# Causal attention: the triangle added by TensorE for all diagonal blocks of the first two query chunks

## The chip, the cores and the metric

The kernel runs on one core of one Trainium2 chip. The metric is the device time of one execution in microseconds (us). The kernel before took 1374.01 us, the median of three runs (1373.12 to 1380.39).

## The reference, cut to what matters

The whole computation has six blocks on 2048 tokens of width 128: a gated feed-forward, a causal attention, the feed-forward again, a mixture of experts, a full attention and the mixture again. The change is in the causal attention alone (16 heads of width 8, all 2048 tokens):

```
scores = jnp.einsum('bhqd,bhkd->bhqk', q, k) * (1.0 / np.sqrt(HD))
causal = (jnp.arange(t)[:, None] >= jnp.arange(t)[None, :]).astype(scores.dtype)
scores = scores * causal - (1.0 - causal) * NEG
attn = jax.nn.softmax(scores, axis=-1)
out = jnp.einsum('bhqk,bhkd->bhqd', attn, v)
```

## The kernel before

The causal attention works in 32 windows: four query chunks `c` of 512 queries, and for each chunk eight pairs of heads, so windows 0 to 7 are chunk 0, 8 to 15 chunk 1, and so on (`Plan.windows`, line 882). Each window is done twice over. First come the row maxima. A `fill` (lines 1245 to 1270) takes one tile of 128 queries, `qt` from 0 to 3, and one key chunk `kc` up to the own one. TensorE computes the scores of both heads into two PSUM banks (line 1262), a head on each half of the array's rows, and VectorE reduces both banks to a maximum per query (lines 1433 to 1443). In the own key chunk only the columns up to the diagonal are computed, so a fill is 128, 256, 384 or 512 wide for `qt` 0 to 3, and its last 128 columns need the triangle that hides later keys. For `qt` 2 and 3 TensorE adds it with four small matmuls (line 1268: identity halves against `hide_q`, accumulated into the same banks), and VectorE does one plain reduction over both banks (line 1441). For `qt` 0 and 1 VectorE does it: one `tensor_tensor_reduce` for each of the two heads adds `mask_q` while it takes the maximum (line 1435); it is a custom operation and a read of the accumulator in the trace. After the last fill of a window one small reduction gives `negmax` (line 1449), POOL splits it into three bf16 parts (lines 1465 to 1471), and TensorE's `turn` adds them to the queries (lines 1281 and 1284), which ScalarE copies to `q_max` (line 1405).

Second come the probabilities, in steps of 128 keys. `scores` (line 1300) fills one of three PSUM banks per head, ScalarE takes the exponential (line 1414), POOL clears what lies under the diagonal of diagonal steps (line 1484), and TensorE multiplies with the values three steps later (`sum_values`, line 1319). ScalarE keeps the sums of a window at the third step of the next (line 1388), and SP sends them to DRAM. Keys and queries of chunk 1 are loaded from DRAM in front of the loop; those of chunks 2 and 3 when the sums of windows 8 and 16 are kept (line 1557).

All engines follow one list, `Plan.order`, written by `in_time` (lines 966 to 1008), a small planner that keeps a clock for TensorE (`tensor`), VectorE (`vector`) and ScalarE (`scalar`), each in us. At each turn it puts down what can start first: a fill (from the time that VectorE's clock minus 1.2 allows), a turn (5 us after the window's maxima), or a step. A fill may be at most six windows ahead of the steps (`AHEAD`). TensorE waits at fill `u` until VectorE has used fill `u - 2` (line 1258), and takes everything in the order of the list. The costs that the planner charges a fill are these:

```
tensor = first + 0.08 + width / 3500.0 + (0.2 if own and late else 0.0)
vector = max(vector, tensor + 0.2) + (0.45 if own and not late else 0.11) + 2 * width / 960.0
```

where `own` says that the key chunk is the query chunk's own and `late` that TensorE adds the triangle. A step costs `tensor` 0.33 us and its columns (up to 512) by 1/4500 + 1/1200 each, and a turn costs it 0.6. The last fill of a window adds 0.2 to `vector`. The full attention further on uses the same classes with `causal` false; its order comes from `in_turns`, and no fill of it is masked.

Of the kernel before, what the change touches and what calls it, by code (L numbers as in the profile page):

```python
# [874 lines left out]
class Plan:  # L875
# [30 lines left out]
    def fills(self, n):  # L906
# [3 lines left out]
            return [(q, j, CW) for j in range(NC) for q in range(TPC)]  # L910
        return [(q, j, CW if j < c else TW * (q + 1)) for q in range(TPC) for j in range(c + 1)]

    def first_query(self, n, kt):

        r = kt - TPC * self.windows[n][1]
        return (TW * r, True) if self.causal and r >= 0 else (0, False)
# [49 lines left out]
    def in_time(self):  # L966


        settle, margin = 5.0, 1.6
        order, tensor, vector, scalar = [], 0.0, 0.0, 0.0  # L970
        maxed, turned, begun = {}, {}, set()
        f = t = turn = 0
        while t < len(self.steps):
            n, i = self.steps[t]
            at_fill = at_turn = at_step = math.inf
            if f < len(self.steps) and self.steps[f][0] < n + self.AHEAD:
                at_fill = max(vector - 1.2, tensor)
            if turn in maxed and (turn < 2 or turn - 1 in begun):
                at_turn = max(maxed[turn] + settle, tensor)
            if n in turned:  # L980
                at_step = max(scalar - 0.5, turned[n] + margin, tensor)
            first = min(at_fill, at_turn, at_step)
            if first == at_turn:
                order.append(("turn", turn, 0))
                turned[turn] = first
                tensor = first + 0.6
                scalar = max(scalar, tensor + 0.2) + 0.6
                turn += 1
            elif first == at_fill:
                m, g = self.steps[f]  # L990
                width = self.fills(m)[g][2]
                order.append(("fill", m, g))
                own, late = self.fills(m)[g][1] == self.windows[m][1], self.fills(m)[g][0] >= 2
                tensor = first + 0.08 + width / 3500.0 + (0.2 if own and late else 0.0)
                vector = max(vector, tensor + 0.2) + (0.45 if own and not late else 0.11) + 2 * width / 960.0
                f += 1
                if g == self.keys(m) - 1:
                    maxed[m] = vector
                    vector += 0.2
            else:  # L1000
                q0, _ = self.first_query(n, i)
                order.append(("exp", n, i))
                begun.add(n)
                tensor = first + 0.2 + (CW - q0) / 4500.0 + 0.13 + (CW - q0) / 1200.0
                scalar = max(scalar, first + 0.5) + 0.3 + 2 * (CW - q0) / 1400.0 + 0.4 / self.keys(n)
                t += 1
        assert f == len(self.steps) and turn == self.count
        return order


class Attention:
# [216 lines left out]
    def pe_loop(self, pe):  # L1228
        ps, k, plan, causal, ST, SUM, MX, NP = self.ps, self.k, self.plan, self.causal, self.ST, self.SUM, self.MX, self.NP
# [15 lines left out]
        def fill(m, f):  # L1245
            u = plan.fill_no[m, f]
            qt, kc, width = plan.fills(m)[f]
            pair, c = plan.windows[m]
            if f == 0:
                operands(m)  # L1250
            if causal and u == 1:
                pe.wait_ge(self.rest_ready, 2 * NC)
            if not causal and m == 0:
                pe.wait_ge(self.k_built, kc + 1)
                if f == 1:
                    pe.wait_ge(self.stage_norm.out, NC * self.stage_ln + NC)
            if u >= 2:
                pe.wait_ge(self.mx_used, u - 1)
            q0 = CW * c + TW * qt
            for j in range(2):  # L1260
                head = slice(HALF * j, HALF * j + HALF)
                mm = pe.matmul(ps[:, MX + 2 * (u % 2) + j, 0:width], q_all[head, pair, q0:q0 + TW],  # L1262
                               k_all[head, pair, CW * kc:CW * kc + width], start=True, stop=True)
            if causal and kc == c and qt >= 2:
                for h in range(2):
                    for j in range(2):
                        head = slice(HALF * j, HALF * j + HALF)
                        mm = pe.matmul(ps[:, MX + 2 * (u % 2) + j, width - TW:width], k["ident_h"][head, h, :],
                                       k["hide_q"][head, h, :], start=False, stop=True, skip_group_check=True)
            mm.then_inc(self.mx_filled, 1)  # L1270
# [149 lines left out]
    def dve_loop(self, dve):  # L1420
        nc, ps, k, plan, MX = self.nc, self.ps, self.k, self.plan, self.MX
        blockmax, negmax = k["blockmax"], k["negmax"]
        for kind, m, f in plan.order:
            if kind == "queries":
                self.dve_rest(dve, m)
            elif kind == "end":
                self.dve_end(dve, m, f)
            if kind != "fill":
                continue
            u = plan.fill_no[m, f]  # L1430
            qt, kc, width = plan.fills(m)[f]
            dve.wait_ge(self.mx_filled, u + 1)
            if self.causal and kc == plan.windows[m][1] and qt < 2:
                for j in range(2):
                    reduce = nc.vector.tensor_tensor_reduce(  # L1435
                        k["hidden"][:, u % 2, j, 0:width], ps[:, MX + 2 * (u % 2) + j, 0:width],
                        k["mask_q"][:, 2 * TW - width:], 1.0, LOWEST, ALU.add, ALU.max,
                        blockmax[:, m % plan.AHEAD, qt, j, kc:kc + 1])
                reduce.then_inc(self.mx_used, 1)
            else:  # L1440
                nc.vector.tensor_reduce(blockmax[:, m % plan.AHEAD, qt, :, kc],  # L1441
                                        ps[:, MX + 2 * (u % 2):MX + 2 * (u % 2) + 2, 0:width], AX.X, ALU.max)\
                    .then_inc(self.mx_used, 1)
            if f == len(plan.fills(m)) - 1:
                dve.wait_ge(self.mx_used, u + 1)
                if m >= plan.AHEAD:
                    dve.wait_ge(self.max_split, 4 * (m - plan.AHEAD + 1))
                blocks = plan.windows[m][1] + 1 if self.causal else NC
                nc.vector.tensor_reduce(negmax[:, m % plan.AHEAD, :, :], blockmax[:, m % plan.AHEAD, :, :, 0:blocks],  # L1449
                                        AX.X, ALU.max, negate=True).then_inc(self.max_ready, 1)  # L1450
                if m % PAIRS == PAIRS - 1 and m > PAIRS:
                    self.dve_invert(dve, m // PAIRS - 1)
# [527 lines left out]
```

## Time and profile before

| what | value |
|---|---|
| median of three runs | 1374.01 us (1373.12 to 1380.39) |
| span of the profiled execution, its own time | 1378.3 us |
| TensorE matmul busy | 1310.4 us, 95% |
| VectorE busy | 1163.7 us, 84% |
| ScalarE busy | 1054.2 us, 76% |
| POOL busy | 164.8 us, 12% |
| masked reductions (L1435) | 128, in the causal attention |
| plain block reductions (L1441) | 768, in both attentions |

The profiled execution is one more execution of the same program; its span is the only time the page has for it. Busy time counts what an engine was at work on; matmuls are pipelined, so their durations overlap and a start to start time says more than a duration. The loop of the causal attention lies between about 85 and 464 us. Idle time is given with what ended it.

### The profile page before, as it was taken

To read this page: it belongs to the slowest core of one execution; us is meant where nothing else is said; L and a number is where in the kernel's file an instruction comes from. 1 tells how busy PE (TensorE), PEld (TensorE's weight loads), DVE (VectorE), ACT (ScalarE), POOL (GpSimd) and SP (SyncE) were. 2 spreads that over 40 slices of the span, in tenths; PEclk is the share of its full clock that TensorE was granted. 3 is DMA by queue.
4 is the path that set the end of the run, shared out by engine and by line. 5 is a ranking of instruction groups with operands and counts; after the bars stand their busy time and mean duration, and the time that the engine had idled before them with its cause. 6 is when DMAs were issued, how large, how long until landed. Compare 5 with 4: busy or idle time off the path is not lost.

```text
span 1378.3 us, 30094 instructions
## 1 busy us (share of the span) xinstructions
PE 1310.4 (95%) x11833; PEld 473.9 (34%) x11896; DVE 1163.7 (84%) x1536; ACT 1054.2 (76%) x2060; POOL 164.8 (12%) x443
## 2 busy tenths in 40 slices
PE   7888999999999898999899999999999999999999
PEld 4343333332333452534233333332333323333533
DVE  6878889999998278555899999999999999995554
ACT  4557888988999546324499999999999999998521
POOL 9234222111111000001000000000000000000000
PEclk9999999999999999899699999999999999999989
DMA  5252301100000012001311000000000000000000
GB/s 147 51 136 40 54 12 36 28 4 12 4 4 4 12 37 56 0 0 52 109 50 49 4 3 12 4 4 3 12 4 3 4 8 9 3 4 3 11 6 25
DMA packets 38524, 35.09 MB, mean 25 GB/s; under 512 B 16080, under 2 KB 31920, under 8 KB 38384
## 3 DMA queue, kind: packets, MB, share of 16 engines
q1 hardware_dynamic: 38384, 33.17, 9.9%
q8 instruction: 94, 1.54, 0.5%
q14 instruction: 46, 0.38, 0.1%
HBM read 17.03 MB, written 9.70 MB: 19 GB/s over the span
## 4 chain that ended last, share of the span: by engine, by line
DVE 32%; PE 21%; issue 1%; ACT 0%; DVEq 0%; ACTq 0%
DVE m_blockmax L1441 31%; PE ps L1323 6%; PE ps L1262 3%; PE ps L1300 3%; PE ps L630 1%; PE ps L619 1%; PE ps L620 1%; PE ps L252 0%; PE ps L245 0%; PE ps L1075 0%; PE ps L1166 0%; PE ps L605 0%; PE ps L648 0%; DVE m_negmax L1449 0%; PE ps L1213 0%
## 5 line engine op out<-in xcount | busy, mean ns | idle before, releaser
L1441 DVE TENSOR_REDUCE m_blockmax<-ps 128x2 f32<-128x1024 f32 (+1 forms) x768 | 880.8, 1207 | 26.6 <-PE ps L1262 18.1
L1414 ACT ACTIVATE m_prob<-ps 128x512 f32<-128x512 f32 (+3 forms) x1664 | 845.9, 577 | 48.0 <-PE ps L1300 33.6
L1300 PE MATMUL ps<-m_q_max,m_k_all 64*128 64x512 bf16 (+3 forms) x1664 | 338.2, 368 | 0.5
L1262 PE MATMUL ps<-m_k_all,m_q_all 64*128 64x512 bf16 (+3 forms) x1664 | 317.8, 380 | 19.9 <-DVE m_blockmax L1441 15.3
L1323 PE MATMUL ps<-m_prob,m_v_op 128*16 128x256 f32 x4096 | 321.0, 385 | 0.1
L1262 PEld LDWEIGHTS ps<-m_k_all,m_q_all 64*128 64x128 bf16 x1664 | 79.8, 93 | 343.2 <-DVE m_blockmax L1441 174.8
L1319 PE MATMUL ps<-m_prob,m_v_op 128*16 128x256 f32 (+3 forms) x2560 | 179.3, 352 | 1.5 <-ACT m_pv L1388 0.8
L1300 PEld LDWEIGHTS ps<-m_q_max,m_k_all 64*128 64x128 bf16 x1664 | 143.3, 94 | 90.5 <-ACT m_prob L1414 47.5
L1323 PEld LDWEIGHTS ps<-m_prob,m_v_op 128*16 128x16 f32 x4096 | 67.4, 94 | 133.5 <-issue 101.3
L1465 POOL CAST m_maxparts<-m_negmax 128x8 bf16<-128x8 f32 x64 | 14.0, 218 | 719.8 <-DVE m_negmax L1449 714.6
L729 ACT ACTIVATE m_prob<-ps 128x512 f32<-128x512 f32 x40 | 23.6, 594 | 74.4 <-PE ps L619 74.4
L1319 PEld LDWEIGHTS ps<-m_prob,m_v_op 128*16 128x16 f32 x2560 | 42.3, 94 | 79.9 <-issue 51.6
L1405 ACT ACTIVATE m_q_max<-ps 128x512 bf16<-128x512 f32 x64 | 38.2, 597 | 38.6 <-PE ps L1284 38.4
L1484 POOL TENSOR_SCALAR_AFFINE_SELECT m_prob<-m_prob 128x256 f32<-128x256 f32 x128 | 51.3, 407 | 129.6 <-ACT m_prob L1414 128.1
L814 DVE TENSOR_TENSOR m_prob<-m_prob,ps 128x512 f32<-128x512 f32 x32 | 22.0, 689 | 32.5 <-PE ps L648 31.6
L1435 DVE CUSTOM_DVE_ANT_0 m_hidden<-ps,m_mask_q 128x256 bf16<-128x256 f32 (+1 forms) x128 | 39.8, 351 | 2.3 <-PE ps L1262 2.0
L260 DVE COPY m_cen<-ps 128x512 f32<-128x512 f32 x28 | 19.0, 685 | 23.3 <-ACT m_sq L288 17.6
L619 PE MATMUL ps<-m_xn,m_e_gate 128*128 128x512 f32 x64 | 35.4, 637 | 2.8 <-DVE m_prob L814 2.6
L292 ACT ACTIVATE m_std<-ps,m_eps 32x128 f32<-32x128 f32 x28 | 10.0, 357 | 34.1 <-PE ps L245 34.1
L1132 POOL TENSOR_TENSOR m_part<-m_sq,m_part 128x512 bf16<-128x512 f32 x8 | 9.2, 1154 | 224.6 <-ACT m_part L1107 224.6
L237 PE MATMUL ps<-m_x,m_centre_of 128*128 128x512 f32 x42 | 25.2, 701 | 10.6 <-DVE m_x L518 5.5
L630 PE MATMUL ps<-m_prob,m_e_down 128*128 128x512 f32 x64 | 35.3, 638 | 0.0
(221 smaller groups left out, 1034.8 us busy)
## 6 DMA issues: line engine op xcount, KB each, us to landing
m_part<-m_xn SPq DMA_DIRECT2D x48, 128.0 KB, 2.3
ba_parts<-m_part SPq DMA_DIRECT2D x8, 384.0 KB, 4.7
ea_parts<-m_part SPq DMA_DIRECT2D x8, 384.0 KB, 2.6
m_k_all<-ea_parts SPq DMA_DIRECT2D x84, 32.0 KB
m_q_all<-ea_parts SPq DMA_DIRECT2D x84, 32.0 KB
m_k_all<-ba_parts SPq DMA_DIRECT2D x36, 64.0 KB
m_q_all<-ba_parts SPq DMA_DIRECT2D x36, 64.0 KB
ba_sums<-m_pv SPq DMA_DIRECT2D x128, 9.0 KB
```

Of the source, the lines that this page charges most:

```text
L237: pe.matmul(self.ps[:, bank, :], self.k["centre_of"][:, :], chunk(src, c), start=True, stop=True)\
L619: pe.matmul(ps[:, i % 2, :], wg, chunk(xn, c), start=True, stop=True).then_inc(self.gate_done, 1)
L630: pe.matmul(ps[:, self.DOWN + m % 2, :], wd, k["hid"][:, i % 2, :], start=(shared or g == 0), stop=(shared or g == GROUPS - 2)).then_inc(s ...
L1262: mm = pe.matmul(ps[:, MX + 2 * (u % 2) + j, 0:width], q_all[head, pair, q0:q0 + TW], k_all[head, pair, CW * kc:CW * kc + width], start=Tr ...
L1300: pe.matmul(ps[:, e % ST, q0:CW], k_all[head, pair, TW * i:TW * i + TW], q_max[m % 2][head, q0:CW], start=True, stop=True).then_inc(self.s ...
L1319: mm = pe.matmul(ps[VC * g:VC * g + VW, SUM, HALF * first:HALF_CW], weights, own, start=(i == 0), stop=True, skip_group_check=True)
L1323: mm = pe.matmul(ps[VC * g:VC * g + VW, SUM, 0:HALF_CW], weights, own, start=(i == 0), stop=True, skip_group_check=True)
L1405: nc.scalar.activation(q_max[m % 2][:, :], ps[:, e % ST, :], ACT.Copy).then_inc(self.st_used, 1)
L1414: nc.scalar.activation(prob[:, (2 * t + j) % NP, q0:CW], ps[:, e % ST, q0:CW], ACT.Exp, scale=SCALE)\
L1435: reduce = nc.vector.tensor_tensor_reduce(k["hidden"][:, u % 2, j, 0:width], ps[:, MX + 2 * (u % 2) + j, 0:width], k["mask_q"][:, 2 * TW - ...
L1441: nc.vector.tensor_reduce(blockmax[:, m % plan.AHEAD, qt, :, kc], ps[:, MX + 2 * (u % 2):MX + 2 * (u % 2) + 2, 0:width], AX.X, ALU.max)\
L1484: pool.affine_select(out=own, in_=own, compare_op=ALU.is_ge, fill=0.0, base=0, pattern=[[0, 2], [1, TW]], channel_multiplier=-1).then_inc( ...
```

## The change

One new function says which fills TensorE masks: those of `qt` 2 and 3 as before, and now also those of `qt` 0 and 1 in windows of chunks 0 and 1. TensorE's fill, VectorE's loop and the planner's costs ask it in place of `qt >= 2` and `qt < 2`.

```diff
+    def masked_by_tensor(self, n, qt):
+
+        return qt >= 2 or self.windows[n][1] < 2
+
...
-                own, late = self.fills(m)[g][1] == self.windows[m][1], self.fills(m)[g][0] >= 2
+                own, late = self.fills(m)[g][1] == self.windows[m][1], self.masked_by_tensor(m, self.fills(m)[g][0])
...
-            if causal and kc == c and qt >= 2:
+            if causal and kc == c and plan.masked_by_tensor(m, qt):
...
-            if self.causal and kc == plan.windows[m][1] and qt < 2:
+            if self.causal and kc == plan.windows[m][1] and not plan.masked_by_tensor(m, qt):
```

## Rows read from the trace of the kernel before

**Rows 1.** The page: the span, and busy time, share and instructions of each engine.
```profile
span 1378.3 us, 30094 instructions
...
PE 1310.4 (95%) x11833; PEld 473.9 (34%) x11896; DVE 1163.7 (84%) x1536; ACT 1054.2 (76%) x2060; POOL 164.8 (12%) x443
```

**Rows 2.** Busy time by stretch of the causal loop, the columns in the second line.
```profile
core 0: us, PE busy (x) PEld busy (x) DVE busy (x) ACT busy (x) POOL busy (x), PEclk, DMA share, GB/s
107.00:133.00 26.00, 23.89 (x340) 9.82 (x344) 22.36 (x57) 21.45 (x59) 13.24 (x45) 1.00 0.20 39
133.00:140.00 7.00, 5.26 (x64) 2.02 (x64) 6.17 (x10) 4.27 (x12) 1.71 (x7) 1.00 0.04 8
140.00:205.00 65.00, 60.67 (x755) 20.98 (x762) 57.80 (x107) 54.64 (x127) 16.82 (x53) 1.00 0.25 35
205.00:218.00 13.00, 10.66 (x124) 3.71 (x124) 12.75 (x20) 8.52 (x21) 2.28 (x8) 1.00 0.02 5
...
328.00:434.00 106.00, 104.80 (x1226) 33.78 (x1224) 103.31 (x139) 97.43 (x204) 15.01 (x48) 1.00 0.03 7
```

**Rows 3.** ScalarE's timeline (start, length): the keeping of a window's sums.
```profile
106.69 0.38 ACT L1388 ACTIVATE m_pv<-ps 128x256 f32<-128x256 f32 x1
...
133.04 0.38 ACT L1388 ACTIVATE m_pv<-ps 128x256 f32<-128x256 f32 x1
139.85 0.39 ACT L1388 ACTIVATE m_pv<-ps 128x256 f32<-128x256 f32 x1
...
204.91 0.41 ACT L1388 ACTIVATE m_pv<-ps 128x256 f32<-128x256 f32 x1
217.50 0.38 ACT L1388 ACTIVATE m_pv<-ps 128x256 f32<-128x256 f32 x1
...
310.63 0.39 ACT L1388 ACTIVATE m_pv<-ps 128x256 f32<-128x256 f32 x1
327.27 0.38 ACT L1388 ACTIVATE m_pv<-ps 128x256 f32<-128x256 f32 x1
```

**Rows 4.** VectorE's timeline, 210 to 214 us: two masked fills and what follows each.
```profile
210.58 0.29 DVE L1435 CUSTOM_DVE_ANT_0 m_hidden<-ps,m_mask_q 128x128 bf16<-128x128 f32 x1 [0.21 <-PE ps L1262]
...
211.01 2.35 DVE L1441 TENSOR_REDUCE m_blockmax<-ps 128x2 f32<-128x1024 f32 x2
213.28 0.41 DVE L1435 CUSTOM_DVE_ANT_0 m_hidden<-ps,m_mask_q 128x256 bf16<-128x256 f32 x1
...
213.96 5.48 DVE L1441 TENSOR_REDUCE m_blockmax<-ps 128x2 f32<-128x1024 f32 x5
```

**Rows 5.** VectorE's plain reductions by shape, 84 to 442 us: busy, mean ns, idle before.
```profile
L1441 DVE TENSOR_REDUCE m_blockmax<-ps 128x2 f32<-128x1024 f32 x224 | 263.5, 1219 | 17.7 <-PE ps L1262 14.0 <-PE ps L1268 1.9
L1441 DVE TENSOR_REDUCE m_blockmax<-ps 128x2 f32<-128x768 f32 x32 | 30.5, 952 | 4.3 <-PE ps L1268 4.0
```

**Rows 6.** The chain that ended last: five full reductions in a row.
```profile
1048.88 5.73 DVE m_blockmax L1441 x5
```

**Rows 7.** Timeline around a masked fill 384 wide: fill, masks, next scores.
```profile
152.48 0.34 PE L1262 MATMUL ps<-m_k_all,m_q_all 64*128 64x384 bf16 x2
...
152.65 0.28 PE L1268 MATMUL ps<-m_hide_q,m_ident_h 64*128 64x128 bf16 x4
...
152.77 0.27 PE L1300 MATMUL ps<-m_q_max,m_k_all 64*128 64x256 bf16 x2
```

**Rows 8.** Timeline, chunk 1: second weight load of the scores behind a fill 128 wide.
```profile
157.39 0.09 PEld L1300 LDWEIGHTS ps<-m_q_max,m_k_all 64*128 64x128 bf16 x1 [0.21 <-ACT m_prob L1414]
```

**Rows 9.** Timeline, chunk 0: the exponentials behind a fill 256 wide issued at 112.06.
```profile
112.60 1.09 ACT L1414 ACTIVATE m_prob<-ps 128x512 f32<-128x512 f32 x2 [0.53 <-PE ps L1300]
```

**Rows 10.** Busy time by stretch, columns as in rows 2; the DMA share is next to last.
```profile
112.00:114.00 2.00, 1.84 (x28) 0.89 (x27) 1.79 (x10) 1.18 (x4) 0.81 (x3) 1.00 0.58 123
114.00:116.00 2.00, 1.93 (x32) 0.78 (x28) 1.95 (x6) 1.95 (x5) 1.38 (x6) 1.00 0.10 20
```

**Rows 11.** TensorE's timeline: the first fill of chunk 1, window 8.
```profile
119.67 0.39 PE L1262 MATMUL ps<-m_k_all,m_q_all 64*128 64x512 bf16 x2 [0.32 <-DVE m_blockmax L1441]
```

## The prediction

> **What bounds the kernel now.** I read the page first, then the busy time by stretch, then the moments at which each window's sums are kept, and last the timeline around single fills. The page [rows 1] shows a span of 1378.3 us with TensorE busy 95% and VectorE 84%. Neither share decides anything here: the change touches only the causal attention, whose loop runs from about 85 to 464 us, and within it only the blocks of chunks 0 and 1. The second attention takes its order from another function and stays as it is, as does all that follows.
>
> By stretch [rows 2]: in chunk 0 (107 to 133 us) and chunk 1 (140 to 205 us) no engine is full. VectorE works 22.36 of 26.00 and 57.80 of 65.00 us, ScalarE 21.45 and 54.64. In chunk 3 (328 to 434 us) VectorE works 103.31 of 106.00 us and sets the pace. Between chunks 0 and 1 (133 to 140 us) ScalarE works only 4.27 of 7.00 us, and between 1 and 2 (205 to 218 us) only 8.52 of 13.00, while VectorE has 12.75 of 13.00. There the planned order issues fills without exponentials, because the first window of the next chunk needs more maxima than are ready: VectorE is late and ScalarE starves.
>
> The keeping of the sums once per window gives these **stalls** a size [rows 3]. Six windows of chunk 0 take 26.35 us, 4.39 each; the seventh interval takes 6.81, of which some 0.2 is that it holds two wider steps: stall 2.2. Seven of chunk 1 take 65.06 us, 9.29 each; the next takes 12.59: stall 3.3. Seven of chunk 2 take 93.13 us, 13.30 each; the next 16.64: stall 3.3. Together 8.8 us. The reader is to see that the loop loses at its chunk borders what VectorE could have done ahead in chunks 0 and 1, where from 107 to 205 us it idles 98.00 - 22.36 - 6.17 - 57.80 = 11.7 us [rows 2].
>
> **The change part by part.** It moves 32 fills (8 pairs, 2 chunks, the query tiles 0 and 1) from a pair of masked reductions on VectorE to four mask matmuls on TensorE and one plain reduction.
>
> VectorE, removed: of a 128 wide fill the pair takes 211.01 - 210.58 = 0.43 us, of a 256 wide one 213.96 - 213.28 = 0.68 us, with the reads of the accumulator inside [rows 4]. Added: a plain reduction over 256 or 512 elements, of which the trace has none. The rows have 1219 ns for 1024 and 952 ns for 768 [rows 5], so 1.04 ns an element; carried on, 418 and 685 ns. In a queue without gaps five of them take 5.73 us [rows 6], that is (5.73 - 1.22) / 4 = 1.13 us apart, 0.09 under the duration. So the new ones cost 0.33 and 0.60 us, and each fill saves 0.10 and 0.08 us: 32 fills, 2.9 us of VectorE. By itself it is off the path in chunks 0 and 1, where VectorE idles 11.7 us, and so worth nothing there. Ends: nothing, and 2.9 us if all of it reaches the path.
>
> TensorE, added: 128 matmuls. Behind a 384 wide fill the first mask starts at 152.65 and the scores behind the fourth at 152.77: 0.12 us for four [rows 7]. Two row halves of the array run side by side. Upper end: the whole 0.28 us of that group's row, since a 128 wide fill hides less of the four weight loads. I take 0.12, as it is a start to start time in the same queue. On the path? In chunk 1 the scores behind a fill mostly wait for ScalarE to free a buffer: the second weight load of the scores at 157.39 waited 0.21 us for it [rows 8], more than 0.12, so there I cost the masks at nothing; the cover is ScalarE's queue, and without it 16 x 0.12 = 1.9 us would come on top. In chunk 0 ScalarE stands idle for 0.53 us until the scores behind a 256 wide fill arrive [rows 9], so there the 8 tiles 1 pay 8 x 0.12 = 1.0, and the 8 tiles 0 half: 0.5. Term: +1.5 us.
>
> The TensorE page of the Trainium skill ("TensorE: Matmul & The Clock Gate", section "Wait - 56ns, not 53.3ns?") speaks against this change: with hardware decode off the sequencer spends about 62 ns on each matmul, which binds when the array's work is shorter. That would be 128 x 62 ns = 7.9 us in place of 32 x 0.12 = 3.8. This trace does not agree: its four matmuls take 0.12 us from start to start.
>
> The order, moved: the planner is told the new costs, and this is the larger part. It charged a masked fill with 0.45 + 2 x width / 960: 0.72 and 0.98 us, where the rows have 0.43 and 0.68. It now charges 0.11 + the same: 0.38 and 0.64, near the 0.33 and 0.60 above. Over 32 fills its VectorE clock falls by 32 x 0.34 = 10.9 us, and its TensorE clock rises by 32 x 0.2 = 6.4. A fill goes into the order when the planned VectorE has at most 1.2 us left, so in chunks 0 and 1 fills move ahead of exponentials. Per window of chunk 0 (fills of 128 + 256 + 384 + 512 = 1280 columns) the planner now sums 2 x 1280 / 960 + 4 x 0.11 + 0.2 = 3.3 us of VectorE against 4.8 of TensorE (before: 4.0 against 4.4), in chunk 1 8.0 against 9.1 (before 8.7 and 8.7). The old order runs 15 fills ahead of the exponentials through chunk 1, 19 through chunk 2 and 23 in chunk 3, and wins the four more at each border by letting the exponentials wait. Now this lead has time to grow before the border. That fills the 11.7 us of VectorE's idle time, and the stalls shrink. I take the first two as gone and the third as halved, because in chunk 2 nothing is cheaper and the lead can only be kept: 2.2 + 3.3 + 1.6 = 7.1 us. What is moved costs TensorE its time in the steady part: some 8 fills at 0.24 us (two halves of 512 columns side by side, against the 2 x 128 columns in 0.12 us above) are now issued between exponentials: 1.9 us. Needed of VectorE: 7.1 of the 11.7 us of idle.
>
> What is late next: TensorE takes fills in order, so a fill ahead of VectorE holds the scores behind it, and ScalarE with them. Fills of chunk 1 need their keys from DRAM. The DMA engines are 0.58 busy from 112 to 114 us and 0.10 from 114 to 116 [rows 10], so that load has landed by 114 to 115; its first fill is issued at 119.67 [rows 11] and would move ahead by some 3 to 4 us. The cover is 1 us thin; without it TensorE stands up to 1 us. POOL's maxima splits, SP's sends and loads are as many as before and follow the same events.
>
> **Sum:** +1.5 (masks) +1.9 (moved fills) -7.1 (stalls) = **-3.7 us**. The profiled execution's span of 1378.3 us is 4.3 above the median of 1374.01, within the runs' 1373.12 to 1380.39; I put the difference on the median: 1374.0 - 3.7 = **1370.3 us**. A measurement of this kernel can tell about 0.5%, 6.9 us, from no change; so this forecast, -0.3%, counts as no change.
>
> **Rivals.**
> Full use of the idle time. The new plan is near the truth for VectorE, so all 11.7 us of idle and the 2.9 us saved turn into an earlier end: 14.6 - 1.5 - 1.9 = 11.2 us, 1362.8. For it: chunk 3 is set by VectorE [rows 2], so what is ahead at its start counts to the end. Against it: the exponentials need TensorE and ScalarE, and their steady periods do not fall. Chance 0.22.
>
> No lead gained. The fills are placed earlier, but TensorE waits for VectorE in front of them and pays at each window what it wins at the border. Then only the masks are left, 0 to 3.8 us, middle 1.5: 1375.5. For it: chunk 0's windows are short chains through four engines. Chance 0.20.
>
> Slower: the narrow fills do not hide the four weight loads and the sequencer, so each of the 32 pays the 0.28 us of the group [rows 7], and VectorE gets its block as much later: 32 x 0.28 = 9.0 us, 1383.0 with no stall won. It decides if the group's time, not the start to start time, is what the next instruction waits for; against it stands 152.77 itself. The Trainium skill's 62 ns a matmul (same page and section) would come to 7.9 us, much the same place. Chance 0.10.
>
> That the change does nothing is excluded: the test holds for every window of chunks 0 and 1, and both loops and the planner ask it.
>
> **How the numbers follow.** Forecast 0.48, with its own range 1366 to 1374 (all three stalls gone, or one of them only). Range: from 1363.0, most of the full use, to 1377.5, the masks with no cover. It leaves out the slower case and a little of the full one. Faster by over 0.5% (under 1367.1): all of full use, 0.22, and 0.12 of the forecast: 0.34. Slower by over 0.5% (over 1380.9): 0.10 and a little for chunk 1's load and a worse order: 0.11. Same: the rest, 0.55.
>
> **What would show it.** Masked custom operations down from 128 to 64; plain reductions 32 more, at 0.42 and 0.69 us. Mask matmuls up by 128. The intervals 6.81 and 12.59 us near 4.8 and 9.5, the third below 16. VectorE's idle time from 107 to 205 us near 5 in place of 11.7. The last sums at about 460 in place of 464.2 us. I am wrong if chunk 0's windows grow by over 0.5 us each, if the stalls stay, or if anything behind the loop moves.

## The result, and the profile after

The changed kernel takes 1388.83 us, the median of 22 runs (1379.39 to 1397.06). Beside them on the same chips the kernel before took 1381.99 us (22 runs, 1373.12 to 1390.36; the three runs that were shown ahead of the prediction lie at the low end of these). The ratio is 1.0046, 95% interval 1.0025 to 1.0066: slower by 0.46%, between 0.25 and 0.66%. The forecast was -0.3%. Of the 18.5 us between its 1370.3 and the measured 1388.83, 8.0 are this difference of the kernel before (1381.99 against 1374.01).

The profile that follows is of the slowest of the 22 executions (1397.06 us).

The page of the changed kernel, its span, engines and two groups of section 5 (the first is VectorE's plain reduction, the second TensorE's fill; behind the bar stand busy time, mean ns and the idle time ahead of them):

```profile
span 1395.3 us, 30317 instructions
...
PE 1326.0 (95%) x12024; PEld 472.2 (34%) x12024; DVE 1163.0 (83%) x1440; ACT 1057.3 (76%) x2060; POOL 165.0 (12%) x443
...
L1445 DVE TENSOR_REDUCE m_blockmax<-ps 128x2 f32<-128x1024 f32 (+3 forms) x800 | 896.8, 1181 | 44.3 <-PE ps L1266 33.3
...
L1266 PE MATMUL ps<-m_k_all,m_q_all 64*128 64x512 bf16 (+3 forms) x1664 | 318.4, 381 | 30.5 <-DVE m_blockmax L1445 20.7
```

VectorE has fewer instructions and as much busy time as before (1163.7) [rows 1], and its reductions now wait longer for fills: of the causal loop, VectorE's plain reductions by shape, 84 to 456 us:

```profile
L1445 DVE TENSOR_REDUCE m_blockmax<-ps 128x2 f32<-128x1024 f32 x224 | 264.6, 1219 | 32.8 <-PE ps L1266 29.3 <-PE ps L1272 2.2
...
L1445 DVE TENSOR_REDUCE m_blockmax<-ps 128x2 f32<-128x512 f32 x16 | 11.0, 687 | 1.4 <-PE ps L1272 1.3
L1445 DVE TENSOR_REDUCE m_blockmax<-ps 128x2 f32<-128x256 f32 x16 | 6.8, 422 | 2.5 <-PE ps L1272 2.2
```

The 224 full reductions take the same 1219 ns each, but 32.8 us of idle time stand ahead of them in place of 17.7 [rows 5]. The two new shapes take 422 and 687 ns, against the 418 and 685 that were worked out.

The keeping of each window's sums in the profile of the changed kernel, which answers to rows 3 (start, length):

```profile
106.78 0.38 ACT L1392 ACTIVATE m_pv<-ps 128x256 f32<-128x256 f32 x1
...
146.54 0.38 ACT L1392 ACTIVATE m_pv<-ps 128x256 f32<-128x256 f32 x1
151.27 0.38 ACT L1392 ACTIVATE m_pv<-ps 128x256 f32<-128x256 f32 x1
...
218.94 0.40 ACT L1392 ACTIVATE m_pv<-ps 128x256 f32<-128x256 f32 x1
228.15 0.40 ACT L1392 ACTIVATE m_pv<-ps 128x256 f32<-128x256 f32 x1
...
326.66 0.38 ACT L1392 ACTIVATE m_pv<-ps 128x256 f32<-128x256 f32 x1
339.71 0.39 ACT L1392 ACTIVATE m_pv<-ps 128x256 f32<-128x256 f32 x1
```

The three border intervals are 4.73, 9.21 and 13.05 us where rows 3 give 6.81, 12.59 and 16.64. The stalls did go, the third one whole. Yet in this execution the first sums come at the same time as before and the last at 479.8 us in place of 464.2: the loop loses more inside its chunks than it wins at their borders. Chunk 0 takes 44.5 us against 33.2. One piece of that is a wait that was not there. TensorE's timeline, the first fill of chunk 1:

```profile
115.43 0.39 PE L1288 MATMUL ps<-m_identb,m_maxparts 128*128 128x128 bf16 x4
122.36 0.61 PE L1266 MATMUL ps<-m_k_all,m_q_all 64*128 64x512 bf16 x2 [6.54 <-DMA m_q_all<-ba_parts]
```

and the same place by stretch (columns as in rows 2):

```profile
114.00:116.00 2.00, 1.81 (x23) 0.55 (x16) 1.33 (x3) 1.58 (x6) 0.77 (x2) 1.00 0.59 79
...
120.00:122.00 2.00, 0.00 (x0) 0.00 (x0) 0.00 (x0) 0.00 (x0) 0.00 (x0) 0.50 0.49 65
...
126.00:128.00 2.00, 2.00 (x16) 0.29 (x15) 1.10 (x3) 0.58 (x3) 0.81 (x2) 0.50 0.13 26
```

The load of chunk 1 lands at about 122 us and not at 114. From 118 to 122 us no engine is busy, and the granted clock falls from 1.00 to 0.50 (from 2.4 to 1.2 GHz) and stays there until about 128 us: the matmul pair takes 0.61 us where it took 0.39.

### The profile page after: what moved, and what is told of

It reads as the page before. It is cut to its first block, busy times and chain, and to the rows that moved or that the text cites. A ratio compares the mean times of both kernels' runs of the same rounds, so it can differ in the third digit from the quotient of the medians.

```text
span 1395.3 us, 30317 instructions
## 1 busy us (share of the span) xinstructions
PE 1326.0 (95%) x12024; PEld 472.2 (34%) x12024; DVE 1163.0 (83%) x1440; ACT 1057.3 (76%) x2060; POOL 165.0 (12%) x443
## 3 DMA queue, kind: packets, MB, share of 16 engines
q1 hardware_dynamic: 38384, 33.17, 10.5%
q8 instruction: 95, 1.56, 0.5%
## 4 chain that ended last, share of the span: by engine, by line
DVE 32%; PE 21%; issue 1%; ACT 0%; DVEq 0%; ACTq 0%
DVE m_blockmax L1445 30%; PE ps L1327 6%; PE ps L1266 3%; PE ps L1304 3%; PE ps L630 2%; PE ps L619 1%; PE ps L620 1%; PE ps L252 0%; PE ps L1170 0%; PE ps L245 0%; PE ps L1079 0%; PE ps L648 0%; PE ps L605 0%; DVE m_negmax L1453 0%; PE ps L1217 0%
## 5 line engine op out<-in xcount | busy, mean ns | idle before, releaser
L1445 DVE TENSOR_REDUCE m_blockmax<-ps 128x2 f32<-128x1024 f32 (+3 forms) x800 | 896.8, 1181 | 44.3 <-PE ps L1266 33.3
L1304 PEld LDWEIGHTS ps<-m_q_max,m_k_all 64*128 64x128 bf16 x1664 | 139.2, 94 | 95.4 <-ACT m_prob L1418 50.9
L1469 POOL CAST m_maxparts<-m_negmax 128x8 bf16<-128x8 f32 x64 | 14.1, 220 | 657.0 <-DVE m_negmax L1453 647.1
L814 DVE TENSOR_TENSOR m_prob<-m_prob,ps 128x512 f32<-128x512 f32 x32 | 22.0, 688 | 33.5 <-PE ps L648 32.8
L260 DVE COPY m_cen<-ps 128x512 f32<-128x512 f32 x28 | 19.1, 687 | 23.3 <-ACT m_sq L288 17.6
L620 PE MATMUL ps<-m_xn,m_e_up 128*128 128x512 f32 x64 | 35.4, 636 | 0.0
```

The costliest lines, as they stand in the source:

```text
L620: pe.matmul(ps[:, 2 + i % 2, :], wu, chunk(xn, c), start=True, stop=True).then_inc(self.up_done, 1)
L1304: pe.matmul(ps[:, e % ST, q0:CW], k_all[head, pair, TW * i:TW * i + TW], q_max[m % 2][head, q0:CW], start=True, stop=True).then_inc(self.s ...
```

## The experiments

Open after this were two questions. Is it the masks on TensorE or the new order that costs time? And what in the order: the load of chunk 1, or something in every window? All ratios below are to the kernel before, run beside it on the same chip, with the 95% interval. The time between the first and the last keeping of sums in each profile (31 windows; the part behind the loop varies by 10 us from one profile to the next, of whatever kernel, from 907 to 917 us) is read beside them. It is of one execution each, and waits for DMA move it by several us: the changed kernel has 373.0 and 364.8, the kernel before 357.5 and 357.2.

| kernel | ratio | first to last sums | window of chunks 1, 2, 3 |
|---|---|---|---|
| before | 1 | 357.5 | 9.07, 13.20, 17.62 |
| changed | 1.0046 | 373.0 | 9.37, 14.15, 18.21 |
| e1 masks, old order | 1.0033 | 364.6 | 9.07, 13.20, 17.62 |
| e2 new order, old masks | 1.0056 | 369.0 | 9.38, 14.15, 18.21 |
| e3 chunk 1's fills held | 1.0033 | 364.9 | 10.31, 13.80, 17.62 |
| e4 fills spread | 1.0037 | 360.2 | 9.38, 13.77, 17.62 |
| e5 two-buffer rule | 1.0016 | 357.7 | 9.21, 13.20, 18.50 and 17.62 |
| e6 masks everywhere, old order | 1.0035 | 362.8 | 9.08, 13.31, 17.73 |
| e7 planner alone | 1.0026 | 360.5 | 9.43, 13.20, 17.62 |
| e8 changed, earlier load | 1.0074 | 371.9 | 9.38, 14.15, 18.21 |
| e9 before, earlier load | 1.0035 | 370.8 | 9.28, 13.20, 17.62 |
| e10 e5, spread from chunk 3 | 0.9997 | 358.5 | 9.21, 13.20, 18.33 and 17.78 |
| e11 e10, earlier load | 1.0036 | 366.1 | 9.22, 13.20, 18.33 and 17.78 |
| e12 before again | 1.0003 | 357.2 | 9.08, 13.20, 17.62 |
| e13 masks again | 1.0012 | 363.7 | 9.07, 13.20, 17.62 |
| e14 changed again | 1.0064 | 364.8 | 9.70, 14.15, 18.21 |
| e15 mixed rule | 0.9983 | 358.1 | 9.21, 13.20, 17.62 |

(A window's time is the median of a chunk's first seven intervals between two keepings; where two times alternate, both stand. The middle intervals of chunks 2 and 3 agree to 0.03 us in most profiles; in chunk 1 of the changed kernel the intervals lie between 8.6 and 11.1 us.)

**e1, the masks alone.** The planner keeps its old costs, so the order is that of before:

```diff
-                own, late = ..., self.masked_by_tensor(m, self.fills(m)[g][0])
+                own, late = ..., self.fills(m)[g][0] >= 2
```

> TensorE adds the triangle for all diagonal blocks of chunks 0 and 1, but the planner keeps its old costs, so the order of the list is that of before. Theory A (the new order costs the time, the masks nearly nothing): the ratio to before is 0.998 to 1.002, the sums of the last window are kept within 2 us of where before has them (464.2 us in its profile), the windows of chunks 2 and 3 stay at 13.2 and 17.6 us. Theory B (the masks cost the time, 0.28 us for each of 32 fills): ratio about 1.0065, 9 us, all of it in chunks 0 and 1, whose windows grow by about 0.5 us.

1.0033 (1.0005 to 1.0061), between the ratios of the two theories, and the last sums come at 472.1 us. The windows of chunks 1 to 3 are those of before. In this profile the loss lies in chunk 0, 40.7 us against 33.2, and most of it is one wait in ScalarE's timeline:

```profile
121.74 0.38 ACT L1392 ACTIVATE m_pv<-ps 128x256 f32<-128x256 f32 x1 [4.93 <-DMA ba_sums<-m_pv]
```

The sums of an earlier window, sent by SP, had not left; the load of chunk 1 landed at about 120 us in this profile. Behind the wait the clock is 0.50 from 122 to 126 us. Whether such a wait is a cost of the masks this run can't tell, so it was repeated as e13.

**e2, the order alone.** The planner of the change, masks and reductions of before:

```diff
-            if causal and kc == c and plan.masked_by_tensor(m, qt):
+            if causal and kc == c and qt >= 2:
...
-            if self.causal and kc == plan.windows[m][1] and not plan.masked_by_tensor(m, qt):
+            if self.causal and kc == plan.windows[m][1] and qt < 2:
```

> The planner has the new costs and writes the new order, but VectorE masks the tiles 0 and 1 everywhere, as before. Theory A (the order): the ratio to before is as high as with the whole change, 1.003 to 1.008; TensorE waits 3 to 8 us at the first fill of chunk 1 for keys and queries from DRAM; windows of chunk 2 take about 14.2 us and of chunk 3 about 18.2, as in the changed kernel. Theory B (the masks): ratio 1.000 or under, since the masks are gone.

1.0056 (1.0034 to 1.0077), with the steady windows of the changed kernel in chunks 1 to 3 to 0.03 us (one of chunk 2 takes 1.1 more), though none of its instructions differs in kind from before. Theory A holds but for the wait for chunk 1's load, which is 2.18 us:

```profile
116.85 0.39 PE L1266 MATMUL ps<-m_k_all,m_q_all 64*128 64x512 bf16 x2 [2.18 <-DMA m_q_all<-ba_parts]
```

**e3, chunk 1's fills held back,** so that the load has landed:

```diff
-                at_fill = max(vector - 1.2, tensor)
+                at_fill = max(vector - 1.2, tensor, 38.0 if self.steps[f][0] >= PAIRS else 0.0)
```

> The whole change, with one line more in the planner: no fill of chunk 1 or later before 38 us on its own clock, which is when the keys had come in the changed kernel's profile. Theory A1 (most of the loss is the wait for the keys and the half clock behind it): the wait of 6.5 us is gone and the kernel is 6 to 12 us faster than the changed one, ratio to before 0.994 to 1.000. Theory A2 (most of the loss is the pattern of fills and steps in chunks 2 and 3): the order of chunk 3 is by this line again that of before, so its windows go back to 17.6 us, but chunk 2 keeps two fills in a row and two steps in a row and stays near 14.1 us; ratio to before 1.001 to 1.005. Theory B (masks): ratio as with the whole change, 1.005.

1.0033 (1.0003 to 1.0063). The wait for the keys is gone, but the held fills come late at the border of chunk 0, whose interval is 11.6 us (6.81 before), and chunk 0 takes 39.3 us against 33.2. As theory A2 expected, chunk 3 takes 17.62 a window again, though the edit holds no fill there; chunk 2 takes 13.80, less than the 14.1 expected. What chunks 2 and 3 cost hangs on where in the window the planner's fills and turns happen to fall, and that is handed down from the chunks before.

**e4, fills spread.** From the first step of chunk 2 on, a fill that follows a fill is held back behind the next step:

```diff
-        self.order = self.with_values(self.in_time()) if causal ...
+        self.order = self.with_values(self.alternate(self.in_time())) if causal ...
```

> The whole change; only from the first step of chunk 2 on is its list put back into strict alternation: never two fills between two steps, and no two steps without a fill while one is held back (206 places differ, the lead stays at 25). Theory P (two fills in a row make TensorE stand in front of a PSUM pair that VectorE still reads, and two steps in a row leave VectorE idle): windows of chunk 2 go from 14.2 to 13.2 us and of chunk 3 from 18.2 to 17.6 us, 10 us of the loop in all; ratio to before 0.996 to 1.000. Theory Q (the larger lead itself slows the windows): 14.2 and 18.2 us stay, ratio 1.005.

1.0037 (1.0012 to 1.0062), above theory P's range. Chunk 3 goes from 18.21 to 17.62, all of the loss there; chunk 2 from 14.15 to 13.77, 0.4 of the 0.95, so theory P holds for chunk 3 and only in part for chunk 2.

**e5, the buffers' own rule.** The planner lets a fill start when VectorE has at most 1.2 us left. TensorE really waits for the end of the reduction two fills back (line 1258). With wide reductions of 1.13 us that is nearly the same thing; with narrow ones of 0.33 and 0.60 us, 1.2 us can hold two reductions, and a fill is planned before its banks are free. So the rule was replaced:

```diff
-        maxed, turned, begun = {}, {}, set()
+        maxed, turned, begun, used = {}, {}, set(), [0.0, 0.0]
...
-                at_fill = max(vector - 1.2, tensor)
+                at_fill = max(used[f], tensor)
...
+                used.append(vector)
```

> The whole change, but the planner lets a fill start when the reduction two fills before it has ended (its own clock), in place of VectorE's clock less 1.2 us; this is the rule by which TensorE really waits. Theory P: alternation holds in chunks 2 and 3 by itself, 13.2 and 17.6 us a window; chunks 0 and 1 lose less than in the changed kernel, since fewer fills are placed in front of a busy buffer: TensorE's idle time in front of fills for VectorE under 12 us in the loop; ratio to before 0.994 to 1.001. Theory Q: no better than the changed kernel.

1.0016 (0.9989 to 1.0044), no longer told from the kernel before. Chunk 0 takes 33.5 us, chunk 1 75.0 (before 77.7), chunk 2 13.20 a window. Chunk 3 stays slow: its windows take 18.50 and 17.62 in turn, 18.06 in the mean, where theory P had 17.6.

**e6, all windows masked by TensorE, old order.**

```diff
-        return qt >= 2 or self.windows[n][1] < 2
+        return True
```

(with the planner's line as in e1)

> The order of before, and TensorE adds the triangle for every diagonal block of all four chunks: 32 masked fills more than with masks alone in chunks 0 and 1. Theory of the prediction (0.12 us each, mostly hidden where VectorE sets the pace): windows of chunk 2 and 3 at 13.2 and 17.6 us or up to 0.2 us below, as VectorE has 0.18 us less to do in each. Theory B (0.28 us each on the path): 13.8 and 18.2 us, another 9 us in the total.

1.0035 (1.0012 to 1.0058). The windows of chunks 2 and 3 go from 13.20 to 13.31 and from 17.62 to 17.73: 0.11 us for two more fills masked by TensorE, 0.055 us each net of what VectorE saves. Neither theory said so: the windows are not shorter, and 0.28 us each would give 0.56. In steady windows this is the cleanest price of the masks. Most of the 5.3 us that the loop takes more than before lies in chunk 0 (38.0 us), which has a wait of 2.84 us of ScalarE for the sums' sends, as in e1.

**e7, the planner alone, masks of before:** e5's rule, and 0.16 in place of 0.45 for what a masked fill costs VectorE beside its columns (two edits in one, so it cannot tell them apart).

> No mask moves: VectorE masks the tiles 0 and 1 as before. The planner has the rule of two buffers and charges these masks 0.16 us over the columns (measured: 0.43 and 0.68 us a pair) in place of 0.45. If the planner's rule is what matters, this is level with the kernel with masks on TensorE and the same rule, ratio to before 0.995 to 1.001. If the masks on TensorE are worth something of their own once the order is right, it is slower than that kernel by 2 us or more.

1.0026 (0.9999 to 1.0054). Chunks 2 and 3 keep their windows, chunk 1 does not, the interval at its border stays (12.30), and that of chunk 2 grows from 16.64 to 18.58. The gain of e5 in chunk 1 does need the cheaper reductions, or another order of fills than this; which of the two is open. At 1.0026 and 1.0016, e7 and e5 are too close to decide between the two expectations.

**e8, e9, e11: chunk 1 loaded earlier,** by the same move in the changed kernel, in the kernel before, and in e10:

```diff
-        if causal:
-            sp.wait_ge(self.parts_sent[1], 16 * 2)
-            load_group(1)
-        else:
+            if causal and i == 3:
+                sp.wait_ge(self.parts_sent[1], 16 * 2)
+                load_group(1)
+        if not causal:
```

> The whole change, and SP sends the parts of chunks 2 and 3 behind the load of chunk 1's keys and queries in place of in front of it (those of chunks 2 and 3 are first read at 150 us). Theory A1 (the new order stands at the first fill of chunk 1 for its keys, for several us and with half the clock behind it, in most executions): the keys come some 3 to 6 us earlier, no wait for DMA at that fill, and the kernel is 3 to 8 us faster than the changed one; ratio to before 0.999 to 1.003. Theory A3 (that wait is rare, and the loss is that windows of chunk 0 hold more fills and those of chunks 2 and 3 have two fills in a row): ratio stays at 1.004 to 1.006.

> Control: the kernel before with the same move of the load alone. Its order reaches chunk 1's first fill some 4 us after the keys have come, so theories A1 and A3 both expect little: ratio 0.997 to 1.000, less where the sending of sums (which in some profiles made ScalarE wait 3 to 5 us behind that load) is freed too.

> The same with the load of chunk 1 moved ahead as well: chunk 1's keys wait for nobody, chunk 0 in 33 us in every execution. Ratio to before 0.992 to 0.999. If it is not under 1.000, what the order gains in chunk 1 (75.0 in place of 77.7 us) is lost again somewhere in chunk 0.

1.0074 (1.0045 to 1.0103), 1.0035 (1.001 to 1.0059) and 1.0036 (1.0009 to 1.0064). All three miss their expectations. The move is bad by itself: the control e9 is slower than before, with a wait of 6.9 us of ScalarE for the sums' sends, the kind of wait seen in e1 (2.1 us in e11), and e8 still waits 3.84 us for the keys. So these three don't price the wait for the keys; e14 shows the loss without it.

**e10, e5 with the fills spread from chunk 3 on.**

> The kernel with the rule of two buffers in the planner and the masks of the change, its list put into strict alternation from the first step of chunk 3 on. Theory P: windows of chunk 3 from 18.06 to 17.62 us, all else as in that kernel; 3 us faster than it, ratio to before 0.996 to 1.001.

0.9997 (0.9973 to 1.0022). The ratio is in the range, but chunk 3 takes 18.33 and 17.78 in turn, the same mean as in e5, so my reading of e4, that a fill on a fill is what costs, fell as a general rule. It was enough in e4 and is not here, where each fill has a step beside it. The lists of one window of chunk 3, as the planners of these kernels write them (E a step of an earlier key chunk, e one of the own, f a full fill, 1 to 4 the own chunk's fills of 128 to 512, T the turn), are:

```
before, 17.62 us  EfEfEfE3EfEfEfE4EfEfEfE1efefeTfe2
e4,     17.62 us  EfEfE3EfEfEfE4EfEfEfE1EfeTfefe2ef
changed 18.21 us  EfEfE3fEfEfE4EfEfEfE1EfEfeTfe2efe
e10, mean 18.05   E2EfEfEfE3EfEfEfE4EfEfEfe1efefeTf
             and  E2EfEfEfE3EfEfEfE4EfEfEfe1efeTfef
```

Which neighbour decides (in e10 the 256 wide fill stands between wide steps) is open. In chunk 2 the lists say more:

```
before, e5, e15, 13.20 us  E3EfEfE4EfEfE1Efefe2eTfef
e4,              13.77 us  E1EfEfE2ETfEfE3Efefe4efef
e3,              13.80 us  EfEfE1EfEfE2ETfEfe3fefee4
changed, e2,     14.15 us  E1EfEfE2ETfEfE3fEfE4eefef
```

All three slow ones have a wide step and the turn between the 256 wide fill and the next one (`2ETf`), where the fast one has a narrow step (`2eTf`). The slowest has two fills in a row (`3f`) and two steps in a row (`ee`) besides, and taking these out is what e4 did.

**e12, e13, e14: before, masks alone and the changed kernel once more,** on one chip. No new edit.

> The kernel before, once more, as if it were another. The ratio is 1.000 within its interval; how far it is off tells what a ratio of 1.003 is worth. If its profile has chunk 0 at 33 us again, the waits for DMA seen in chunk 0 with masks on TensorE and the old order belong to the masks; if it has 36 us or more with a wait for DMA, they come with the time at which chunk 1's load lands and not with the masks.

> Masks in chunks 0 and 1 with the order of before, again. If masks cost 4 us, the ratio is 1.003 again. If the windows in the profile tell the whole (0.05 us a fill, 2 us in all at most), it is 1.000 to 1.002.

> The changed kernel again: ratio 1.003 to 1.007. Windows of chunks 2 and 3 at 14.15 and 18.21 us in every execution, since they come from the order; TensorE's wait for chunk 1's keys between 0 and 7 us, since it comes from when the DMA lands.

1.0003 (0.9972 to 1.0035), 1.0012 (0.9986 to 1.0039) and 1.0064 (1.0031 to 1.0096). In e13 the masks alone can't be told from nothing; chunk 0 with them takes 33.7 us against 33.2. But e1 is the same kernel and was 1.0033, so what the masks cost is not settled: the middle of the two, 1.0022, is 3 us. e12's chunk 0 takes 33.1 us without a wait for DMA. By the expectation that would lay the waits of e1 and e6 on the masks, but e13 has none and e9, with masks on VectorE, has the longest: open. (One interval of chunk 1 in e13 is 5.7 us longer than the others: TensorE stands for 2.92 us until 173.03 with no releaser in the trace, and the clock is 0.50 from 174 to 178 us. e9 has such a stand, 3.85 us at 178.7.) e13 and e14 ran side by side and differ in the planner's line alone; their medians, 1380.41 and 1387.87, are 7.5 us apart. And e14's profile shows the changed kernel without the wait for the keys, the first fill of chunk 1 in TensorE's timeline:

```profile
115.83 0.39 PE L1266 MATMUL ps<-m_k_all,m_q_all 64*128 64x512 bf16 x2
```

Its keeping of sums:

```profile
106.86 0.38 ACT L1392 ACTIVATE m_pv<-ps 128x256 f32<-128x256 f32 x1
...
142.86 0.38 ACT L1392 ACTIVATE m_pv<-ps 128x256 f32<-128x256 f32 x1
...
220.07 0.41 ACT L1392 ACTIVATE m_pv<-ps 128x256 f32<-128x256 f32 x1
234.22 0.41 ACT L1392 ACTIVATE m_pv<-ps 128x256 f32<-128x256 f32 x1
...
318.53 0.38 ACT L1392 ACTIVATE m_pv<-ps 128x256 f32<-128x256 f32 x1
331.58 0.39 ACT L1392 ACTIVATE m_pv<-ps 128x256 f32<-128x256 f32 x1
...
471.65 0.38 ACT L1392 ACTIVATE m_pv<-ps 128x256 f32<-128x256 f32 x1 [0.98 <-PE ps L1323]
```

From these and rows 3, with 464.2 us for the last sums before: chunk 0 takes 36.0 us against 33.2 (+2.8), chunk 1 77.2 against 77.7 (-0.4), chunk 2 111.5 against 109.8 (+1.7), chunk 3 140.1 against 136.9 (+3.2). That is +7.3 us from the first to the last sums. From the first fill on VectorE to the first sums it takes 22.8 against 21.3 (+1.5; the other profiles that start with this order have 21.9 to 23.3). Together +8.8 us; e14's ratio of 1.0064 is as much, 8.8 us of 1379, and that the two agree so well is luck, since one is of single executions. The spans of these two, 1381.0 and 1378.3 us, are only 2.7 apart, because the part behind the loop took 909.3 us in e14 and 914.1 before.

By stretch, chunk by chunk (columns as in rows 2), first e14:

```profile
107.00:143.00 36.00, 32.04 (x460) 13.24 (x456) 30.52 (x38) 26.38 (x71) 15.01 (x51) 1.00 0.05 11
143.00:220.00 77.00, 71.60 (x907) 24.55 (x907) 69.73 (x93) 62.85 (x143) 19.84 (x64) 1.00 0.21 30
220.00:332.00 112.00, 108.08 (x1252) 33.51 (x1249) 101.50 (x149) 97.43 (x211) 18.11 (x60) 1.00 0.14 21
332.00:441.00 109.00, 105.70 (x1230) 33.31 (x1230) 103.16 (x139) 98.99 (x204) 15.00 (x48) 1.00 0.03 6
```

then before:

```profile
107.00:140.00 33.00, 29.15 (x403) 11.84 (x408) 28.53 (x66) 25.72 (x70) 14.95 (x51) 1.00 0.17 32
140.00:218.00 78.00, 71.33 (x876) 24.69 (x886) 70.56 (x126) 63.16 (x146) 19.10 (x61) 1.00 0.21 30
218.00:328.00 110.00, 106.34 (x1259) 35.50 (x1266) 105.08 (x158) 96.66 (x209) 19.82 (x64) 1.00 0.10 21
```

VectorE's idle time (length minus its busy time) is 5.5, 7.3, 10.5 and 5.8 us in e14, and 4.5, 7.4, 4.9 and (328 to 434) 2.7 us before [rows 2]. Together it grew from 19.5 to 29.1 us. TensorE's waits for VectorE in front of fills, 84 to 480 us (total, times, longest) in e14:

```profile
PE ps L1266 <- DVE m_blockmax L1445: 17.2, 37, 0.9
```

and before:

```profile
PE ps L1262 <- DVE m_blockmax L1441: 9.8, 21, 1.0
PE ps L1262 <- DVE m_blockmax L1435: 1.7, 5, 0.6
```

**e15, the masks of the change with a mixed rule:** the buffers' rule up to chunk 2, the old one in chunk 3:

```diff
-                at_fill = max(vector - 1.2, tensor)
+                at_fill = max(used[f] if self.steps[f][0] < 3 * PAIRS else vector - 1.2, tensor)
```

> Masks of the change; the planner lets a fill start by the rule of two buffers for windows of chunks 0 to 2, and by the old rule for those of chunk 3. By its list, chunks 2 and 3 have the old patterns, so 13.2 and 17.62 us a window, and chunk 1 takes 75.0 us as with two buffers: 2.7 us less than before in the loop. Ratio 0.995 to 1.000.

0.9983 (0.9957 to 1.0009): 1378.24 us against 1379.21 before, and 0.7% under the changed kernel that ran beside it (1387.87). TensorE's waits for VectorE in front of fills in its profile:

```profile
PE ps L1267 <- DVE m_blockmax L1446: 6.5, 15, 0.9
```

and its keeping of sums in chunk 2 and at its border:

```profile
216.94 0.41 ACT L1393 ACTIVATE m_pv<-ps 128x256 f32<-128x256 f32 x1
230.14 0.41 ACT L1393 ACTIVATE m_pv<-ps 128x256 f32<-128x256 f32 x1
...
310.05 0.39 ACT L1393 ACTIVATE m_pv<-ps 128x256 f32<-128x256 f32 x1
327.57 0.38 ACT L1393 ACTIVATE m_pv<-ps 128x256 f32<-128x256 f32 x1
```

The windows of chunks 2 and 3 are as short as before (13.20, 17.62) and chunk 1 takes 75.0 us, 2.7 less. Chunk 0 takes 35.6 (2.4 more, of which 2.0 is one stand of TensorE with no releaser), and the border of chunk 2 costs 17.52 in place of 16.64 [rows 3]. What is won at one border is again paid elsewhere, and e15 doesn't beat the kernel before by an amount that can be measured. It does win back the changed kernel's loss with the masks in place.

## Why the prediction was wrong

**The masks: right.** The estimate was 0.12 us for four of them behind a narrow fill. The changed kernel's TensorE timeline, a fill 128 wide, its masks and the next fill:

```profile
104.19 0.23 PE L1266 MATMUL ps<-m_k_all,m_q_all 64*128 64x128 bf16 x2
104.25 0.28 PE L1272 MATMUL ps<-m_hide_q,m_ident_h 64*128 64x128 bf16 x4
104.36 0.27 PE L1266 MATMUL ps<-m_k_all,m_q_all 64*128 64x256 bf16 x2
```

0.11 us. On the path they cost +0.5 us in chunk 0 (e13) where +1.5 was put down, nothing in chunk 1's steady windows (9.07, e13), and 0.055 us a fill in the steady windows of chunks 2 and 3 (e6). Whether they also bring on waits such as that of e1 is open. The slower rival, 0.28 us each and 9.0 us in all, had the sign and nearly the size of the result by a mechanism that did not take place; so had the 62 ns a matmul that the Trainium skill states for hardware decode off ("TensorE: Matmul & The Clock Gate", "Wait - 56ns, not 53.3ns?"): four matmuls at that price are 0.25 us, and the row has 0.11. Whether decode was off in these runs is not on record.

**The stalls at the borders: right, and more.** 7.1 us were to go, the third stall by half; in e14 the intervals shrink by 2.1, 3.4 and 3.6 us, 9.1 together.

**The step that failed** is the one behind it: "What is moved costs TensorE its time in the steady part: some 8 fills at 0.24 us". It took the windows inside the chunks for constant but for TensorE's time for the moved fills, 1.9 us, and the masks' 1.5. Adding the lost and won parts, they grew by 8.8 + 9.1 = 17.9 us in e14, in place of 3.4: 1.5 ahead of the first sums, 4.9 in chunk 0, 3.0 in chunk 1, 5.3 in chunk 2, 3.2 in chunk 3. Chunk 0's windows alone grew by 0.8 us each, over the 0.5 that the prediction had named as the sign of being wrong. Nor is it some 8 fills: the lead in the planner's list is 16 to 21 fills in chunk 0, up to 27 in chunk 1 and 25 from there on, where the old list has 12, 15, 19 and 23. The new list could have been counted before any run. In the same step, "That fills the 11.7 us of VectorE's idle time" was the wrong picture of idle time: e14 has 12.8 us of it in chunks 0 and 1, 16.3 in chunks 2 and 3 (7.6 before). A fill that is placed earlier in the list only runs earlier if its banks are free (line 1258 of the kernel before). TensorE takes the list in order, so otherwise it stands, holds the scores behind the fill, and VectorE gets its next fill no sooner. In e14's timeline, in chunk 0:

```profile
100.59 0.28 PE L1266 MATMUL ps<-m_k_all,m_q_all 64*128 64x256 bf16 x2 [0.51 <-DVE m_blockmax L1445]
...
107.77 0.28 PE L1266 MATMUL ps<-m_k_all,m_q_all 64*128 64x256 bf16 x2 [0.71 <-DVE m_blockmax L1445]
```

The prediction saw this ("a fill ahead of VectorE holds the scores behind it") and gave it no term of the sum. The rival "No lead gained" was nearest in mechanism, but let the loop pay at most what it wins.

**What is shown and what is argued.** Shown: the order alone costs as much as the whole change (e2 1.0056, changed 1.0046 and 1.0064), and the masks alone less (e1 1.0033, e13 1.0012, though e1's interval overlaps e2's). The same masks with the two orders, e13 and e14, are 7.5 us apart. That the masks cost nothing is not shown. Shown: replacing the planner's 1.2 us rule brings back chunk 2's 13.20 and cuts TensorE's waits for VectorE from 17.2 to 6.5 us (e5, e15). Shown: chunks 2 and 3, where nothing is cheaper, lose 0.95 and 0.59 us a window through the new list, with the masks of before (e2) as with the new ones; the prediction looked at chunk 2's lead and never at what its windows would look like. In chunk 2 of the changed kernel TensorE issues a wide step's scores, values and a turn between two fills:

```profile
285.82 0.28 PE L1266 MATMUL ps<-m_k_all,m_q_all 64*128 64x256 bf16 x2
285.94 0.65 PE L1304 MATMUL ps<-m_q_max,m_k_all 64*128 64x512 bf16 x2
286.52 0.62 PE L1323 MATMUL ps<-m_prob,m_v_op 128*16 128x256 f32 x8
287.08 0.39 PE L1285 MATMUL ps<-m_q_all,m_identb 128*128 128x512 bf16 x1
...
287.62 0.39 PE L1266 MATMUL ps<-m_k_all,m_q_all 64*128 64x512 bf16 x2
```

and VectorE, with only the narrow fill's masked pair to do meanwhile, stands:

```profile
288.05 2.36 DVE L1445 TENSOR_REDUCE m_blockmax<-ps 128x2 f32<-128x1024 f32 x2 [1.03 <-PE ps L1266]
```

It stands twice more in the same window, around the two fills and the two steps in a row (282 to 298 us):

```profile
283.99 2.36 DVE L1445 TENSOR_REDUCE m_blockmax<-ps 128x2 f32<-128x1024 f32 x2 [0.27 <-PE ps L1266]
...
295.10 2.36 DVE L1445 TENSOR_REDUCE m_blockmax<-ps 128x2 f32<-128x1024 f32 x2 [0.22 <-PE ps L1266]
```

In the kernel before VectorE stands at the turn too, but half as long, and nowhere else by over 0.2 us in such a window (250.5 to 265 us):

```profile
253.49 6.62 DVE L1441 TENSOR_REDUCE m_blockmax<-ps 128x2 f32<-128x1024 f32 x6 [0.52 <-PE ps L1262]
```

So the window loses 0.51 us at the turn and 0.27 + 0.22 at the other two places, 1.00 in all where 0.95 was measured. e4 bears this out: with fills and steps in alternation the two small stands are gone, and the one at the turn stays:

```profile
295.52 3.22 DVE L1462 TENSOR_REDUCE m_blockmax<-ps 128x2 f32<-128x1024 f32 x3 [0.92 <-PE ps L1283]
```

That moving the turn alone would win back the rest was not run. Open: which neighbour decides in chunk 3 (e4 against e10).

**The keys of chunk 1.** "The cover is 1 us thin; without it TensorE stands up to 1 us." The cover was sized from one execution: the five profiles with this order or its start (changed, e2, e4, e8, e14) have waits of 6.54, 2.18, 0, 3.84 and 0 us. Load and wait vary from execution to execution, and a wait of 6.5 us brings the half clock with it. It explains the profile's span, not the verdict: 8.8 us are lost without it in e14, and the ratio of 1.0046 is 6.4 us of 1382 (3.5 to 9.1). How much it adds on average is open.

**Behind the loop** no edit shows: 914.1 us before, 915.5 after, and e12, the same kernel as before, 915.3. Over all profiles this part varies from 907 to 917 us, so a shift of under some 10 us there could not be seen in one.

## What to carry to other kernels

Where an order is planned from a cost table, making one operation cheaper in the table can shift the phase of everything behind it, also in stages that the edit leaves alone: compare the two lists, window by window, before counting anything as constant. A planner's rule for when work may be issued that was fitted to long operations can fail when they become short; the buffers' own rule made chunk 1 faster and brought chunk 2 back here, and left chunk 3 slower than before (e5), so it is no cure for all. And build the operation and the order as two kernels at once, since their costs have different sizes: here most of the loss was the order's.

## What the runs showed of the hardware

The granted clock fell from 1.00 to 0.50 after TensorE had stood for some 3 us (0.63 in the stretch from 118 to 120 us, 0.50 in the next), was still 0.50 at 128 us, after 5.6 us of work, and was 1.00 again from 130 us. In e2 TensorE stood for 2.18 us only, with 1.56 us of work from 114 to 118 us; its clock was 0.50 from 120 to 122 us, while it was busy throughout.

The load of chunk 1, the same transfers behind the same events, landed at about 108 us in e14, 111 in e4, 114 before, 116 in e15, 120 in e1 and 122 in the changed kernel's first profile (where the DMA share falls). A cover of a few us read from one profile says little here. SP sends the sums behind this load, and in e1, where it was late, ScalarE waited 4.93 us for such a send.
